# Four DMA transposes move from SyncE's queue to ScalarE's, the first tile is quantised ahead of ctx, and three tile turns move one group on

## What is computed

```python
def fake_quant(x, scale, zp):                # 8 bits, 0..255
    q = clip(round(x / scale + zp), 0, 255)
    return (q - zp) * scale

x = x + fake_quant(layernorm(x)) @ fake_quant(ctx)          # layer one, per batch

h = layernorm(x).astype(bfloat16)                           # layer two
qg, sg = dynamic_quant(h, inv_gate)     # xs = h*inv; scale = max|xs|/127 per row; q = round(xs/scale)
qu, su = dynamic_quant(h, inv_up)
gate = (qg @ w_gate.T) * sg * s_gate
up   = (qu @ w_up.T) * su * s_up
inter = clip(silu(gate) * up, -10, 10).astype(bfloat16)
qi, si = dynamic_quant(inter, inv_inter)
x = x + (qi @ w_down.T) * si * s_down
```

## Time and profile before

| | before |
|---|---|
| median of 3 runs | 996.07 us (995.58 to 997.15) |
| the profiled execution's own time | 991.43 us |
| its span in the trace | 989.7 us |
| TensorE busy, of the span | 927.1 us, 94% |
| VectorE busy | 691.4 us, 70% |
| ScalarE busy | 352.4 us, 36% |
| GpSimd busy | 241.5 us, 24% |

### The profile page before, as it was taken

One profiled execution on the slowest core, in us unless ns is written; L12 is line 12 of the kernel. 1 busy time (PEld: TensorE's weight loads), 2 busy tenths in 40 slices (PEclk: granted clock), 3 DMA queues, 4 the chain that ended last, 5 costly groups with the idle time before them and its releaser, 6 DMA issues.

```text
span 989.7 us, 11475 instructions
## 1 busy us (share of the span) xinstructions
PE 927.1 (94%) x4316; PEld 420.5 (42%) x4316; DVE 691.4 (70%) x1020; ACT 352.4 (36%) x275; POOL 241.5 (24%) x239
## 2 busy tenths in 40 slices
PE   1799979999997889999999999999999999999998
PEld 0444434444442333444444444444444444444443
DVE  5777266358599888989997777877738795444444
ACT  3756258465647732333332333322234610000000
POOL 2318465535464022333332221111200000000000
PEclk9999999999998998999999999999999999999999
DMA  8795796866869603333443333333267913974222
GB/s 351 270 404 133 258 368 242 354 247 210 277 248 358 211 13 84 96 96 97 100 99 88 96 97 96 96 83 88 51 246 224 326 57 114 349 250 138 85 85 85
DMA packets 123479, 177.43 MB, mean 179 GB/s; under 512 B 102816, under 2 KB 102816, under 8 KB 105760
## 3 DMA queue, kind: packets, MB, share of 16 engines
q1 hardware_dynamic: 118672, 142.62, 45.0%
q10 hardware_dynamic: 4752, 34.08, 8.7%
HBM read 113.77 MB, written 37.75 MB: 153 GB/s over the span
## 4 chain that ended last, share of the span: by engine, by line
PE 71%; DVE 9%; DMA 8%; issue 5%; POOL 4%; ACT 2%; SPq 1%; ACTq 0%; DVEq 0%; POOLq 0%
PE ps L1127 41%; PE ps L1139 22%; PE ps L1107 6%; DMA ctx_stage<-in_ctx 4%; DVE w_slots L841 2%; DMA w_raw<-in_w_gu 2%; DMA q1T<-x_q 2%; POOL x_tile L682 2%; DVE small_operands L766 1%; PE ps L1076 1%; DVE small_operands L872 1%; DVE ctx_u L739 1%; POOL small_operands L649 1%; SPq L295 1%; DVE x_tile L792 1%
## 5 line engine op out<-in xcount | busy, mean ns | idle before, releaser
L1127 PE MATMUL ps<-w_slots,qT_even 128*128 128x512 f16 x1024 | 228.4, 385 | 13.3 <-issue 12.9
L1107 PE MATMUL ps<-ctx_slot,q1T 128*128 128x512 f16 x1024 | 227.8, 383 | 7.4 <-DVE q1T L746 3.6
L1127 PE MATMUL ps<-w_slots,qT_odd 128*128 128x512 f16 x1024 | 224.7, 381 | 7.0 <-issue 6.9
L1139 PE MATMUL ps<-w_slots,qiT 128*128 128x512 f16 x1024 | 221.2, 379 | 0.0
L1127 PEld LDWEIGHTS ps<-w_slots,qT_even 128*128 128x128 f16 x1024 | 101.1, 99 | 139.3 <-issue 21.7
L1127 PEld LDWEIGHTS ps<-w_slots,qT_odd 128*128 128x128 f16 x1024 | 100.4, 98 | 129.9 <-issue 6.0
L1107 PEld LDWEIGHTS ps<-ctx_slot,q1T 128*128 128x128 f16 x1024 | 100.5, 99 | 129.4 <-DVE q1T L746 4.4
L1139 PEld LDWEIGHTS ps<-w_slots,qiT 128*128 128x128 f16 x1024 | 100.2, 98 | 120.8
L531 ACT ACTIVATE q_f<-q_i 128x2048 f16<-128x2048 int8 x32 | 61.1, 1910 | 147.2 <-DVE q_i L853 147.2
L922 DVE SCALAR_TENSOR_TENSOR down_tmp<-ps,small_operands,down_scales_b 128x512 f32<-128x512 f32 x64 | 48.0, 749 | 92.2 <-PE ps L1139 92.2
L682 POOL TENSOR_TENSOR x_tile<-x_tile,col_bias 128x512 f32<-128x512 f32 x64 | 92.1, 1462 | 29.1 <-DVE x_tile L792 26.7
(11 more groups left out here) (94 smaller groups left out, 702.0 us busy)
## 6 DMA issues: line engine op xcount, KB each, us to landing
ctx_stage<-in_ctx ACTq DMA_DIRECT2D x32, 1024.0 KB, 7.7
x_scratch<-x_tile SPq DMA_DIRECT2D x16, 1024.0 KB, 6.2
w_raw<-in_w_gu SPq DMA_DIRECT2D x16, 1024.0 KB, 9.1
x_tile<-x_scratch SPq DMA_DIRECT2D x16, 1024.0 KB, 9.0
x_tile<-in_x SPq DMA_DIRECT2D x15, 1024.0 KB, 11.2
x_and_xs<-x_scratch SPq DMA_DIRECT2D x15, 1024.0 KB, 5.1
out_x<-x_tile SPq DMA_DIRECT2D x15, 1024.0 KB, 5.1
w_raw<-in_w_dn SPq DMA_DIRECT2D x8, 1024.0 KB, 10.2
```

The lines of the kernel that those rows point to most:

```text
L1107: last = nc.tensor.matmul(ps[:, bank(g), :], q1T[m][:, k, :], ctx_s[j % 4][:, k, :], start=(k == 0), stop=(k == KT - 1))
L1127: last = nc.tensor.matmul(ps[:, bank(S2 + i), :], qT[t % 2][:, which, k, :], wsl[:, unit(p, k // 4), hl, k % 4, :], start=(k == 0 and hl = ...
L1139: last = nc.tensor.matmul(ps[:, bank(S3 + i), :], qiT[t % 8][:, k, :], wsl[:, unit(4 + c, k // 4), hl, k % 4, :], start=(k == 0 and hl == ...
```

## The change

Three edits:

1. `transpose_q` for tiles 0 and 1 leaves SP's list. ScalarE issues the same DMA transpose itself, right behind the `cast_q` that fills its source, behind the same wait as before (the store of tile 12 for tile 0, `h_bf16(1)` for tile 1). SP's own transposes begin with tile 2.
2. VectorE quantises tile 0 right after ctx quad 0 and ahead of the statistics of tile 1; ScalarE casts tile 0 ahead of ctx quad 0.
3. TensorE turns tile 8 in group 26 instead of 25, tile 9 in 28 instead of 27, tile 10 in 30 instead of 29. Tile 11 stays in 31. VectorE's `turn_out` moves along.

```diff
-        turn_at = {-1: 0, 0: 1, 1: 2, 2: 3, 25: 8, 27: 9, 29: 10, 31: 11}
+        turn_at = {-1: 0, 0: 1, 1: 2, 2: 3, 26: 8, 28: 9, 30: 10, 31: 11}
...
             def transpose_q(which, t):
                 sp.wait_ge(q16_ready[which], t + 1)
-                if t == 0:
-                    sp.wait_ge(x2_stored[12 % 8], 32)
-                elif t == 1:
-                    sp.wait_ge(hb_ready, 2)
-                else:
-                    sp.wait_ge(pe_done, S2 + at2[t - 2, 2 + which] + 1)
+                sp.wait_ge(pe_done, S2 + at2[t - 2, 2 + which] + 1)
                 sp.dma_start_transpose(qT[t % 2][:, which, :, :], q16[:, :]).then_inc(qT_ready[which][t % 2], 16)
...
             load_x2(1)
-            transpose_q(0, 0)
             sp.wait_ge(pe_done, chunk_end[6])
             load_w(2, 0)
             load_w(2, 1)
             sp.wait_ge(pe_done, chunk_end[7])
             load_w(2, 2)
             load_w(2, 3)
-            transpose_q(1, 0)
             store_x2(13)
             store_x2(15)
             load_w(3, 0)
-            transpose_q(0, 1)
             store_x2(14)
             for g, m in ((1, 15), (2, 13)):
                 sp.wait_ge(x2_stored[m % 8], 32)
                 load_w(3, g)
-            transpose_q(1, 1)
             sp.wait_ge(x2_stored[14 % 8], 32)
             load_w(3, 3)
             load_x2(2)
...
                 nc.scalar.activation(q16[:, :], q8[:, :], ACT.Copy).then_inc(q16_ready[which], 1)
                 act.wait_ge(q16_ready[which], t + 1)
                 act.sem_inc(q8_cast, 1)
+                if t < 2:
+                    if t == 0:
+                        act.wait_ge(x2_stored[12 % 8], 32)
+                    else:
+                        act.wait_ge(hb_ready, 2)
+                    act.dma_start_transpose(qT[t][:, which, :, :], q16[:, :]).then_inc(qT_ready[which][t], 16)
...
             act.wait_ge(scalars_ready, 1)
+            quantise_x(0)
             cast_quad(0)
-            quantise_x(0)
             cast_quad(1)
             quantise_x(1)
...
             quant_quad(0)
+            quantise_x(0)
             ln1_stats(1)
-            quantise_x(0)
             quant_quad(1)
             quantise_x(1)
             turn_out(0)
```

## The result

| | before | after |
|---|---|---|
| median | 995.83 us (991.91 to 997.15, 4 runs) | 1031.22 us (1025.57 to 1035.85, 4 runs) |
| profiled execution / span | 991.43 / 989.7 us | 1030.07 / 1028.3 us |
| TensorE busy | 927.1 us, 94% | 925.4 us, 90% |

The recorded ratio is 1.0381 [1.0347, 1.0415]; the two medians of the table alone give 1.036 (35.4 us). Either way it is far outside my range (up to 1004.0). The two profiled executions differ by 38.6 us. TensorE computes as long as before, so this is waiting. (VectorE is 16.0 us busier, 707.4 for 691.4; its sixteen smoothing passes took 61.8 us in all and 42.9 before.

A forecast was written before the change was run, and what follows sets the result against it. VectorE, with ScalarE's steps ahead of it, was taken to bound stage two's start, TensorE's waits being cover. Terms -2.1 + 0.3 + 4.35 = +2.55 us, added to the 996.07 median, gave 998.6 us; range 993.2 to 1004.0.

The forecast's parts named there:

- Part 1, the turns: Stage one, TensorE's turns of tiles 8 to 11: one group later saves waits, 2.1 us gained (bounds 0 and 3.45).
- Part 2: Start of stage one, tile 0 quantised first: first matmul slightly later, 0.3 us lost (bounds 1.3 lost, 0.5 gained).
- so the 2.1 us reach stage two whole: End of stage one: evacuations, stores and loads follow TensorE's groups, so the turns' 2.1 us gain carries fully into stage two.
- Part 3, the transposes: Start of stage two, four transposes issued by ScalarE: 1.25 + 3.3 - 0.2 = 4.35 us lost.
- ScalarE's queue is empty: Issue time of a transpose on ScalarE: 3.3 us taken, between ends of 1.3 and 7.1 us.
- Tile 0 gate: ScalarE's first transpose, tile 0's gate rows: more than 3 us free behind it, so no cost.
- Its weight loads come up to 2 us earlier: SP freed of four issues: loads up to 2 us earlier for weight part 2, some 10 for part 3's last; 0.2 us gained.
- Tile 0 up: ScalarE's transpose of tile 0's up rows: 3.3 us issue less 2.05 slack costs 1.25 us (ends 0 and 5).
- Tile 1 up: ScalarE's transpose of tile 1's up rows, ahead of `w_hi`: whole issue delays VectorE, 3.3 us (ends 1.3 and 7.1).
- ScalarE's queue starves: Rival at stage two's start: transposes take 6.34 and 7.14 us as behind a backlog; +9.4 us, 1005.5 us, chance 0.14.
- The issue is cheap: Rival: each transpose issue takes 1.9 us on ScalarE's empty queue; sum -0.1, 996.0 us (994.9 to 997), chance 0.26.
- The issue does not hold ScalarE: Rival: `w_hi` starts beside tile 1's up-rows issue; sum -2.0, 994.1 us, down to 992.6, chance 0.20.

The follow-up runs named there:

- the mirror: The kernel before, with ScalarE issuing the four loads of weight part 2 and the four transposes staying on SP: 993.08 us, one execution, beside 993.28.
- SP held: The change, but SP waits at the four places where it used to issue transposes until ScalarE's transpose has landed: 1004.85 us, ratio 1.0119.
- 2 KB rows: The change, with loads of weight parts 2 and 3 and stores of tiles 13 to 15 cut into four DMAs of 512 columns: 1014.3 us, one execution.
- stores beside: The change, but SP issues three stores only after the first transpose landed, and the loads of weight part 2 after the second: 1007.81 us, one execution.
- one queue: The change, but ScalarE also issues weight part 2's four loads ahead of its first transpose; SP issues nothing until two transposes landed: 1009.90 us beside 991.95.
- stage one's two edits alone: The kernel before with edits 2 and 3 only (first tile ahead of ctx, turns one group later), transposes still on SP: 992.92 us, ratio 0.9983.
- the turns alone: The kernel before with only the change's table of turns (tiles 8, 9, 10 one group later): 992.41 us beside 993.28, ratio 0.9986.

## Why the prediction was wrong

**Part 1, the turns: right in the mechanism,** as far as stage one goes. I forecast 3 us of waiting at tile 9's turn, 1.3 to 2 at tile 11's, and stage one 1.8 us shorter. Measured in the trace after: 3.09, 1.13 and 1.73. The 1.73 is in part luck, as stage one ends anywhere from 291.80 to 296.60 with this table, and at 292.19 in the mirror with the old one. Better is the stretch with the turns, from 112.59 before and 113.02 after to the end of stage one: 181.35 and 179.19 us, 2.16 less for a forecast of 2.1. Even that is no fixed gain: in three of the eleven traces the stretch takes 180.8 to 180.9, and in the mirror, with the old table, 179.62. **Part 2: right in direction.** 23.2 was forecast for the first matmul; it came at 23.54, 0.56 later than before, inside the bounds (0.3 was forecast). But "so the 2.1 us reach stage two whole" was wrong. `h_bf` of tile 0 runs 1.7 us earlier, the cast behind it only 0.6, since VectorE's smoothing pass in between took 3.42 us where it took 2.29:

```profile
280.73 3.42 DVE L858 TENSOR_TENSOR x_and_xs<-h_bf,inv_gate_b 128x2048 f32<-128x2048 bf16 x1 [0.43 <-ACT h_bf L510]
```

The wait of the cast was 4.36 or 4.37 us in six of the fourteen traces (before, SP held, 2 KB rows, mirror, stores beside, one queue) and 5.49 or 5.50 in the other eight, nothing between, so this is no fixed price of the change. GpSimd works beside VectorE there; that this is what stretches the pass was not tried.

**Part 3, the transposes: +4.35 forecast, +38.6 there.** The failed steps are these; the second and third carry most of the loss.

- "ScalarE's queue is empty, which speaks for 1.92 ... I take 3.3 us." The issues took 19.95, 8.34, 1.78 and 3.68 us. My upper end of 7.1 came from issues behind a backlog in the same queue, and I held that the worst. Beside traffic of the other queue it was worse: 19.95 us. VectorE's idle time before its low halves, forecast at over 4 us, was 3.23; the delay had come in before it.
- "Tile 0 gate: ScalarE has more than 3 us free behind it. Nothing." This line carries 30.1 of the 38.6 us. It was true of an issue of 3 us. I gave no price to its upper end, though `h_bf(1)` and the cast of the up rows stand behind it.
- I priced the issue and never the landing. The landing of 37.9 us, not the issue of 19.95, ends the wait of the next cast, as `q_f` is one buffer. The front of this document had that sentence; the sum did not use it.
- "Its weight loads come up to 2 us earlier", booked as a gain of 0.2. They came 4 us earlier (288.79 for 292.77) and thereby stood beside the transpose and not behind it. The last load of part 3, forecast some 10 us earlier, was not earlier: SP issued the last three from 327.96 to 333.15, the last one before at 328.84, as the stores ahead of them now took 15 to 27 us to land.
- Tile 0 up: 1.25 us forecast, the issue was 8.34 and all of it counted, as the slack of 2.05 had gone. Tile 1 up: 3.3 forecast, 0.17 for both of tile 1's.

**The rivals.** *ScalarE's queue starves* was the right mechanism, with a chance of 0.14 and +9.4 us. The reason given there (small packets beside large) fits the first landings with shorter rows and not the second. It was priced with issue times alone. The kernel in which SP is held ended at 1004.85, next to its 1005.5. That is near what starved issues cost when no landing is stretched beyond 11 us; but that kernel lost 11.4 us to its own before, some of it in stage one, so the match is in part chance. *The issue is cheap* is true for the one case in which nothing runs beside it (2.10, 1.78 us). Two of the ends stated are off, and nothing hangs on them: by its own terms the cheap case at 1.3 us gives 995.4 and not 994.9, and the next rival with 3.45 us gives 992.7 and not 992.6. *The issue does not hold ScalarE* is refuted: idle 20.18 us, ended by the issue. Of the Trainium skill's rules the one on turns between queues pointed the right way, and that issue time is "usually small relative to the DMA itself" ("DMA: Bandwidth & Descriptors", section "Issuing engines are not separate DMA queues") did not hold here: 19.95 of 37.9 us. (The prediction had set an issue of 7.14 us against the load behind it; its own DMA landed 9.2 us after its start.)

## What to carry to other kernels

Before a small-packet DMA such as a transpose moves to another engine's queue, look at what will stand beside it in the other queue: here it landed when that had drained, or later, and the order within one queue had protected it. Price its issue and its landing separately, follow each to what is behind it (the sequencer's next instruction; the buffer that it frees), and price both at the far end of the range, above all at the places where the near end costs nothing. Here nothing was to be won: stage one's two edits alone, 0.9983 [0.9965, 1.0001], and the turns alone, 0.9986 [0.9966, 1.0007], can't be told from no change.

## What was not expected of the hardware

- A transpose of 0.52 MB lands in 4.4 us alone and in 8 to 38 us beside 2 to 8 MB of other transfers: 7.9 to 37.9 on ScalarE's queue, 14.5 in the one case with it on SP's and the loads on ScalarE's. Its issue holds the sequencer for about 2 us in the one case and 3.4 to 20 in the other.
- Beside it the stores suffer too: 23.4 us to landing (median) in the kernel after, 5.3 in the same stretch before.
- With transposes on ScalarE's queue and 8 KB rows on SP's the engines moved 70 and 74 GB/s at a share of 1.35 and 1.20, though SP's queue had stores and loads under way. With the queues exchanged it was 410, with nothing but loads under way. No run tells why.
